# Two-layer scan network with mixtures of experts: two-part gate broadcasts, row sums on GpSimd, one gate transpose, new orders, no products of the unit matrix

## The reference, cut to what matters

```python
def conv(x, in_w, in_b, out_w, out_b, gamma, beta):      # 64 channels -> 32 heads x 2 x 2 states
    inp, og, fg = jnp.split(x @ in_w + in_b, 3, axis=-1)
    inp, og, lam = silu(inp), sigmoid(og), sigmoid(fg)
    inp_f = (1 - lam) (x) inp                            # outer product inside each head of 2
    s = bidir_scan(rows: inp_f, lam) + bidir_scan(columns: inp_f, lam)   # h_t = lam_t h_(t-1) + inp_t
    out = einsum('...hde,...hd->...he', s, og)
    return layernorm(out) * gamma + beta @ out_w + out_b
x = x + conv0(ln(x));  t = ln(x)
# layer 0: 16 experts, best two; hidden = silu(t @ w1[e]) * (t @ w2[e]);  out = hidden @ w3[e], 64-128-64
x = x + sum_e gate0[e] * out_e
x = x + conv1(ln(x));  t = ln(x)
# layer 1: 8 experts, best two; gelu(t @ W1[e] + b1[e]) @ W2[e] + b2[e], 64-256-64
x = x + sum_e gate1[e] * out_e
```

## Time and profile before

| | us |
|---|---|
| median of 3 runs (244.5 to 246.68) | 244.7 |
| the profiled execution | 244.31 |
| its span, first to last instruction | 242.4 |
| PE busy | 223.8 |
| DVE busy | 185.9 |
| ACT busy | 173.7 |
| POOL busy | 129.4 |

### The profile page before, as it was taken

One profiled execution on the slowest core, in us unless ns is written; L12 is line 12 of the kernel. 1 busy time (PEld: TensorE's weight loads), 2 busy tenths in 40 slices (PEclk: granted clock), 3 DMA queues, 4 the chain that ended last, 5 costly groups with the idle time before them and its releaser, 6 DMA issues.

```text
span 242.4 us, 4082 instructions
## 1 busy us (share of the span) xinstructions
PE 223.8 (92%) x1108; PEld 144.5 (60%) x1108; DVE 185.9 (77%) x539; ACT 173.7 (72%) x407; POOL 129.4 (53%) x208
## 2 busy tenths in 40 slices
PE   6999598869999996999999999999999999999991
PEld 6898597647556562584645655566456636663540
DVE  4778599999999995599978999973894896324133
ACT  5768699779856454874378943789999997885540
POOL 7048686825958764541488441898261635616022
PEclk9979979979999999999999999999999999999997
DMA  1199900083930694930690004300005200080440
GB/s 38 19 233 183 181 0 3 0 173 89 201 67 0 127 205 105 202 68 5 141 207 4 1 0 105 74 0 1 0 3 128 47 0 5 5 193 0 106 115 22
DMA packets 18547, 18.54 MB, mean 76 GB/s; under 512 B 5351, under 2 KB 12285, under 8 KB 18525
## 3 DMA queue, kind: packets, MB, share of 16 engines
q1 hardware_dynamic: 18524, 18.28, 37.2%
...
## 4 chain that ended last, share of the span: by engine, by line
PE 34%; ACT 14%; DMA 14%; issue 11%; DVE 10%; POOL 9%; SPq 7%; POOLq 1%; ACTq 0%; DVEq 0%
PE SPARE L1323 10%; PE SPARE L1465 9%; PE SPARE L1324 9%; DMA gates_b<-gates_dram 8%; DMA up_raw<-in_L_ffn_w_dram 5%; PE SPARE L1339 4%; POOL total L590 4%; ACT hidden L977 3%; SPq L607 2%; DVE hidden L1237 2%; ACT hidden L963 2%; DMA gates_dram<-gates_t 2%; ACT lam_fh L910 1%; SPq L614 1%; POOL up_lo L746 1%
## 5 line engine op out<-in xcount | busy, mean ns | idle before, releaser
L1323 PE MATMUL SPARE<-tok_z,up_hi 128*128 128x512 f32 x192 | 81.9, 427 | 2.4 <-ACT silu_h L957 0.8
L1324 PE MATMUL SPARE<-tok_z,up_lo 128*128 128x512 f32 x192 | 76.2, 397 | 0.0
L590 POOL TENSOR_TENSOR total<-total,weighted 128x512 f32<-128x512 f32 x39 | 50.0, 1282 | 26.2 <-DVE weighted L1260 13.6
L1465 PE MATMUL SPARE<-hidden,down 128*64 128x512 f32 x256 | 60.9, 603 | 0.3 <-ACT hidden L977 0.3
L957 ACT ACTIVATE silu_h<-SPARE 128x512 f32<-128x512 f32 x64 | 37.6, 598 | 25.1 <-PE SPARE L1324 23.2
L1323 PEld LDWEIGHTS SPARE<-tok_z,up_hi 128*128 128x128 f32 x192 | 36.4, 190 | 24.9 <-issue 9.7
L1237 DVE TENSOR_TENSOR hidden<-silu_h,SPARE 128x512 f32<-128x512 f32 x64 | 42.3, 675 | 3.3 <-ACT silu_h L957 3.0
L1324 PEld LDWEIGHTS SPARE<-tok_z,up_lo 128*128 128x128 f32 x192 | 36.5, 190 | 5.7
L1465 PEld LDWEIGHTS SPARE<-hidden,down 128*64 128x64 f32 x256 | 15.9, 136 | 31.2 <-issue 25.4
L1336 PE MATMUL SPARE<-ident 128*128 128x128 f32 x168 | 26.1, 318 | 2.5 <-POOL ident L689 1.9
L1336 PEld LDWEIGHTS SPARE<-ident 128*128 128x128 f32 x168 | 25.2, 233 | 3.2 <-POOL ident L689 1.9
...
## 6 DMA issues: line engine op xcount, KB each, us to landing
gates_b<-gates_dram SPq DMA_DIRECT2D x6, 1024.0 KB, 9.9
gates_b<-gates_dram SPq DMA_DIRECT2D x8, 512.0 KB, 6.1
...
up_raw<-in_L_ffn_W_dram SPq DMA_DIRECT2D x2, 512.0 KB, 6.6
...
down<-in_L_ffn_w_dram SPq DMA_DIRECT2D x1, 512.0 KB, 10.2
down<-in_L_ffn_W_dram SPq DMA_DIRECT2D x1, 512.0 KB, 4.4
```

The costliest lines, as they stand in the source:

```text
L590: nc_engine.tensor_tensor(t, t, weighted[:, q % WEIGHED_RING, :], ALU.add).then_inc(s_sum, 1)
L1323: nc.tensor.matmul(dst, hi, z, start=True, stop=False)
L1324: return nc.tensor.matmul(dst, lo, z, start=False, stop=True)
L1465: last = nc.tensor.matmul(spare("down", q)[k * D:(k + 1) * D, :], w, hidden[:, at, :], start=(j == 0), stop=(j == chunks - 1))
```

## The change

- **Gate broadcasts in two parts for every unit.** `first_gates(u)` is 2 pairs for unit 0 as before, and half of the pairs for the others. The first half signals `s_gback`, the second `s_grest`; the first `weigh` waits for the one, the `weigh` in the middle for the other.
- **Row sums on GpSimd.** `sum_w` of chunks 2 to 8 moves from DVE to POOL. For these chunks the backward row scan writes to `lam_rw` in SBUF instead of PSUM, since POOL adds from SBUF, and a memset on POOL puts the zeros back into `lam_rw` afterwards.
- **One gate transpose.** The gates lie as 64 (or 32) columns, and one transpose to 64 (32) rows of 128 takes the place of four. The copy and the transfer to DRAM have the shape 64 x 128 (32 x 128).
- **Waits.** ACT and DVE leave out waits that a former wait covers, each with its own list of what it has heard. Where a stage has several waits, the order of them is changed.
- **Loads.** The rows of groups 1 to 3 are loaded before the vectors and the small weights. The load of layer 1's up weights follows the first unit's broadcast.
- **New orders and banks** on all engines.
- **No products of the unit matrix**: `BUSY_BEFORE` and `keep_busy` are gone.

```diff
+SUM_BY_POOL = (2, 3, 4, 5, 6, 7, 8)
+SUM_WAYS = "w"
-FIRST_GATES = 2
+def first_gates(u):
+    return 2 if u == 0 else PAIRS[layer(u)] // 2
...
 ORDER = {
     "PE": (
-        "a_turn0 a_turn1 b_turn0 p_f0 p_i0 v_turn0 p_o0 p_f1 p_i1 p_o1 products0 a_turn2 heads0 p_f2 p_i2 p_o2 "
+        "a_turn0 a_turn1 b_turn0 p_f0 p_f1 p_i0 v_turn0 p_o0 p_i1 p_o1 products0 a_turn2 p_f2 p_i2 p_o2 a_turn3 "
...
-BUSY_BEFORE = (
-    "a_turn0:10 a_turn1:1 products0:7 a_turn2:25 heads1:3 p_f3:7 a_turn4:12 e_turn0:7 logits0:2 up_a0:7 up_a1:2 "
-    "up_b1:1 ")
...
-        gates_t = sb("gates_t", [16, TOK])
+        gates_t = sb("gates_t", [16 * TILES, P])
...
             for l in range(LAYERS):
                 load_vector(l, 0, conv_in_b[l], s_in_b)
+            load_rows(1, GROUPS, s_x[1])
...
-            load_rows(1, GROUPS, s_x[1])
             load_up(0)
...
-                loads = ((0, FIRST_GATES, s_gfirst), (FIRST_GATES, e // 2, s_gback[0])) if u == 0 else ((0, e // 2, s_gback[u % 2]),)
-                for first, end, s in loads:
+                for first, end, s in ((0, first_gates(u), s_gback[u % 2]), (first_gates(u), e // 2, s_grest[u % 2])):
                     for k in range(2):
                         sp.dma_start(gates_b[k * D:(k + 1) * D, u % 2, first:end, :],
...
+            def sum_scans(way, c):
+                scanned, fwd = (s_scan_w, fwd_w) if way == "w" else (s_scan_h, fwd_h)
+                back = lam["r" + way]
+                pool.wait_ge(scanned, c + 1)
+                nc.gpsimd.tensor_tensor(fwd[:, places(c)], fwd[:, places(c)], back[:, places(c)],
+                                        ALU.add).then_inc(s_pool_sum[way], 1)
+                pool.wait_ge(s_pool_sum[way], pool_sums_before(c) + 1)
+                nc.gpsimd.memset(back[:, SEQ - 1:TOK:SEQ], 0.0).then_inc(s_padded[way], 1)
...
             def scan_rows_back(c):
-                nc.vector.tensor_tensor_scan(bank[:, ::-1], lam["rw"][:, places(c)][:, ::-1], bank[:, ::-1], 0.0, ALU.mult,
+                out = lam["rw"][:, places(c)] if summed_by_pool("w", c) else bank
+                nc.vector.tensor_tensor_scan(out[:, ::-1], lam["rw"][:, places(c)][:, ::-1], bank[:, ::-1], 0.0, ALU.mult,
...
             def hidden_product(n):
-                dve.wait_ge(s_silu_h, STEP_AT[n] + 1)
-                dve.wait_ge(s_upb, n + 1)
-                if frees_hidden(n) is not None:
-                    dve.wait_ge(s_dn, frees_hidden(n) + 1)
+                if unheard("up_b", n):
+                    dve.wait_ge(s_upb, n + 1)
+                if frees_hidden(n) is not None and unheard("down", first_of_group(frees_hidden(n))):
+                    dve.wait_ge(s_dn, last_of_group(frees_hidden(n)) + 1)
+                if unheard("act", n):
+                    dve.wait_ge(s_silu_h, STEP_AT[n] + 1)
...
-            def keep_busy(kind, u):
-                wait_spare(kind, u)
-                for _ in range(BUSY[kind, u]):
-                    nc.tensor.matmul(spare(kind, u)[:, 0:P], ident[:, :], ident[:, :], start=True, stop=True)
...
-                for t in range(TILES):
-                    last = turn(spare("g_turn", u)[0:e, t * P:(t + 1) * P], gates[:, t, 0:e])
-                last.then_inc(s_gateturn, 1)
+                turn(spare("g_turn", u)[0:e * TILES, 0:P], gates[:, 0:e * TILES]).then_inc(s_gateturn, 1)
```

256 lines of the change are left out of this document (161 added, 95 removed), and 172 rows, old and new, of tables (BANK_USES, ORDER).

## The result

The changed kernel takes **242.04 us** (median of 20 runs, 240.82 to 243.38), the kernel before 243.81 (20 runs beside it, 242.44 to 246.68). The ratio is **0.9934, 95% interval 0.9909 to 0.9959**: 1.6 us faster (1.0 to 2.2). The profiled execution took 241.51 us with a span of 239.3, against 244.31 and 242.4. Forecast were 239.0 and a fall of 5.5 us, so the sign was right and the size was not. Of the 20 timed executions of the changed kernel 17 have a lower mean granted clock (0.94 to 0.964) than the profiled one (0.971).

What follows compares the result with a forecast made beforehand. PE and DVE were taken to bound most of layer 0 together, PE alone layer 1. From 244.31 us, -3.0 - 2.5 - 1.0 + 1.0 = -5.5 gave 238.8, forecast as 239.0 us for the median; 8-in-10 range 234 to 245.

Steps and rivals of the forecast that it cites:

- The start: Up to DVE's first expert product: 4.3 us of pauses gained less 1.3 for low clock, 3.0 us gained.
- The term: Start: PE at 1.2 GHz delays hand-overs on DVE's chain, 0.3 us per chunk, 1.3 in all (bounds 0 and 5).
- no cause any more: Start: DVE's pauses of 1.10, 0.88 and 2.35 us, laid to ACT waiting for up weights, all vanish: 4.3 us gained.
- Layer 0: Layer 0's experts: row sums leave DVE, the gate wait goes, PE saves transposes; 2.5 us gained (bounds 0 and 5.3).
- half of DVE's 5.0 us: Layer 0: DVE sheds up to 5.0 us, half lands, since after each wait PE or DVE finds the other busy.
- Layer 1: Layer 1: PE is the bound, and single gate transposes save 4 x 0.26 = 1.0 us (bounds 0.5 and 1.3).
- Only PE's own work counts: Layer 1: PE alone sets the time, so the 6.76 us wait for the last gates gives zero.
- POOL: POOL's seven row sums are covered, but one collision holding up a DVE instruction loses 1.0 us (bounds 0 and 6.7).
- rival 2: POOL becomes the one waited for; DVE stands at the sum of both scans in each chunk: 242.7 us, chance 0.14.
- Rival 3: Start gains nothing lasting: POOL splits and low clock hold first experts; or first half-broadcast is no earlier. 241.7 us, chance 0.18.
- Rival 1: The clock stays at 1.2 GHz until 60 us, costing 6.6 us more between 40 and 60: 247.5 us, chance 0.11.
- The signs I named: Included first expert product by 45 us, DVE pauses before 28 us below 7, DVE busy near 182 in layer 0.

Runs made afterwards that it cites:

- Experiment 1: Changed kernel with products of the unit matrix put back where PE stood idle in the first 44 us: 238.94 us, ratio 0.9819 to the kernel before.
- experiment 2: Kernel before with only its products of the unit matrix taken out: ratio 1.0103 to the kernel before.
- experiment 12: Changed kernel with products of the unit matrix only ahead of stages up to p_f3 (first 26 us): ratio 0.9849 to the kernel before.
- 9: Changed kernel with products of the unit matrix, more of them where PE still stood idle, up to up_a2: ratio 0.985 to the kernel before.
- Experiment 5: Kernel before with only the gate broadcasts split in two parts for every unit: ratio 0.9911 to the kernel before.
- experiment 3: Changed kernel with the row sums of chunks 2 to 8 back on DVE, none on POOL: ratio 0.9997 to the kernel before.
- experiment 7: Changed kernel with 20 products of the unit matrix added to PE's work in layer 0: ratio 1.0004 to the kernel before.
- experiment 15: Changed kernel with products of the unit matrix and four gate transposes in place of one: ratio 0.9864 to the kernel before.
- experiment 8: Changed kernel with 20 products of the unit matrix added to PE's work in layer 1: ratio 1.0017 to the kernel before.
- 16: Changed kernel with products of the unit matrix, and value7 moved behind weigh32 and x_res3 in DVE's list: 238.82 us, ratio 0.9797 to the kernel before.
- 17: Changed kernel with products of the unit matrix, value7 moved later and value8 moved behind weigh35 in DVE's list: 238.77 us, ratio 0.9792.
- experiment 4: Changed kernel with each gate broadcast whole again for all units but the first: ratio 1.039 to the kernel before.
- 6: Changed kernel with every wait of ACT and DVE issued again, none left out: 241.71 us, ratio 0.9887 to the kernel before.

## Why the prediction was half right

**The start (forecast -3.0, or -2.0 with the +1.0 of POOL, whose collision fell here; measured +0.97 in the pair of profiles).** This step failed, and it holds the whole error. I had named its failure as a condition: the first expert product no earlier. The waits for up weights that I took for the cause of the three pauses are gone, and still the 4.3 us were not gained, for two reasons.

- *The low clock took 2.6 us, not 1.3.* Experiment 1 shows it (46.21 for 48.83), experiment 2 prices it in the old order (2.5 timed, 1.4 at the first product). The term was 0.3 us for each of four chunks, on the hand-overs I had listed. I left out the two longest pieces of PE work in DVE's way. One is the small products: 3.9 us at 1.2 GHz, ahead of chunk 2's transpose in PE's list, with `biases0` now right behind chunk 4's statistics in DVE's. The other is what stands ahead of unit 0's logits, 4.2 us. By experiment 12 they share the 2.6 us about evenly. The total of 11 us more PE work was on the page; about a quarter of it landed. My bound of 5 held it.
- *The order gives 1.65 us with the clock high (46.21 for 47.86), not 4.3.* DVE's pauses up to its first expert product fall from 11.02 to 8.03 us, so 3.0 go and not 4.3: "no cause any more" did not hold for all three. The 0.88 us ahead of chunk 2's input are 1.28 us here, with ACT behind chunk 2's transpose and no longer behind weights:

```profile
23.45 0.70 DVE L1207 SCALAR_TENSOR_TENSOR SPARE<-tanh_f,SPARE 128x512 f32<-128x512 f32 x1 [1.28 <-ACT SPARE L936]
```

And DVE does 1.3 us more work ahead of that product (38.18 for 36.84 us): `in_w1`, 0.90 us, stands ahead of it now, POOL holds up four instructions for 2.95 us in all where it was three for 1.59, and one sum of 0.67 is gone. I counted pauses and not what is in the list.

On the clock the rule of the Trainium skill ("TensorE: Matmul & The Clock Gate", section "Why this matters for your kernels") was the better guide: keep the engine without gaps. The runs agree, with 2.5 us in one order and 2.6 in the other. But experiments 1 and 9 also show low clock that costs nothing (47 to 51 us), where DVE was busy without a break.

**Layer 0 (forecast -2.5, measured -2.25).** The mechanism was right in its parts: DVE sheds work and the wait for gates is gone. That half of DVE's 5.0 us landed is luck in part. Experiment 5 shows most of the wait landing (2.1 of 2.61 us in layer 0), and experiment 3 all of DVE's work (2.3 for the 1.8 of three sums). Something in the new order gives some back: DVE waits 5.0 us more for `silu_h`, and the split alone already made layer 0 2.1 us shorter. Which part of the order does it was not tested. For added PE work it is somewhat under half (1.8 of 4.5, experiment 7).

**Layer 1 (forecast -1.0; measured -1.8 from the 64th product to the end).** The single transpose gives 0.6 of my 1.0 (experiment 15). The rest comes with the order, and was not taken apart. "Only PE's own work counts" does not hold: added work landed by six tenths (experiment 8). The one wait of DVE that was moved there counted for nothing (16, 17), but the longer waits for gates of experiment 4 went with 2.1 us more.

**POOL (forecast +1.0).** Right for the collision: one with a sum, 0.99 us, in the start. The cast of `parts_e` took 1.22 us beside it, and 0.23 alone. Against the kernel before this one is nothing new, since a split held the same cast there; what is new is the subtraction behind the second cast, 1.39 us for 0.29, beside a split that starts at 38.55 us. It is there in experiment 3 too, so it comes from the order and not from the sums:

```profile
34.25 1.22 DVE L1181 CAST parts_e<-norm_e 128x128 fp32r<-128x128 f32 x1
...
38.31 0.23 DVE L1181 CAST parts_e<-norm_e 128x128 fp32r<-128x128 f32 x1
38.58 1.39 DVE L1182 TENSOR_TENSOR parts_e<-norm_e,parts_e 128x128 f32<-128x128 f32 x1
```

```profile
34.12 1.27 POOL L785 TENSOR_TENSOR fwd_w<-fwd_w,lam_rw 128x512 f32<-128x512 f32 x1 [1.13 <-DVE lam_rw L1221]
```

A second instruction, the `pick` at 47.08, was held for 0.41 us with a sum and a split beside it, as with a split alone before. No expert product or weighing was held at a sum for more than 0.2 us, as the Trainium skill has it for one operand in PSUM ("SBUF — State Buffer", "Who interferes with whom"). DVE waited for POOL's sums 0.95 us in all, so rival 2 did not come.

**The sum.** 244.7 less 5.5 is 239.2; the 239.0 of the forecast is a slip of 0.2 us. The three stages measured here (+0.97, -2.25, -1.8) add up to the 3.1 us between two single profiles, while the timed runs give 1.6, so each of them is good to about 1 us. That the start is later does not rest on one pair: five profiles with this start (the changed kernel's, and experiments 4 and 6 to 8) have the first expert product at 48.33 to 49.95 us, the kernel before and experiment 5 at 47.86 and 47.61.

**The rivals.** Rival 3 has the number, 241.7 us, and its first half is near to what happened: the start gains nothing and the low clock is why. But DVE was not earlier first, as it says, and its first expert product waited for no split. Its other half is refuted (experiment 5: the first part of a broadcast does come earlier). Rival 1 did not come in this profile; the clock was high from 44.5 us. It came in part in the profiles of experiments 3, 4, 7 and 12, low again for 6.8 us, and cost some 0.5 us there and not 6.6. I gave the two cases in which the low clock eats the start 0.29 together, and those in which it doesn't 0.57; I had read ACT's list behind the pauses and not PE's. The signs I named for DVE's busy time (182.0), ACT without waits for up weights, and PEclk 0.50 until 44.5 us all came, and did not tell the forecast from rival 3. Those that did were the first expert product, and DVE's pauses before 28 us: 9.1 us, below 7 in the forecast and 10.2 before.
